# Writing the zero rows in front of the experts' regions later and in pairs, in an AdaLN mixture-of-experts block

## The chip, the cores and the metric

One core of a Trainium2 chip runs the kernel. The metric is device time in microseconds (us) of one launch, taken as the median of the runs shown. On the engines: TensorE is PE in the profile (its weight loads PEld), VectorE is DVE, ScalarE is ACT, GpSimd is POOL, and SyncE is SP, which here only issues DMAs.

## The reference

The input x has 16 steps of 256 tokens of 256 features. For each sample a small stencil with three coefficients makes `du`; the block then works on `du` as a sequence of 16 steps:

```python
hn = layernorm(x); qkv = hn @ in_proj_w.T + in_proj_b
scores = einsum('sbnd,tbnd->bnst', q, k) / 4          # causal over the 16 steps, 16 heads
x1 = x + softmax(scores) @ v @ out_proj_w.T + out_proj_b
hn2 = layernorm(x1); rp = softmax(hn2 @ router_w.T)   # 8 experts
topw, topi = top_k(rp, 2)                             # gates
y = sum over the 2 chosen experts of gate * gelu(hn2 @ w1[e]) @ w2[e]
out = input + x1 + y
```

## The kernel before

The 4096 tokens are 32 blocks of 128, one per iteration of a loop that every engine writes out for itself (`for g in range(-AHEAD, G + 3)`, with `G = 32` and `AHEAD = 4`). The work is software-pipelined. In iteration g, POOL makes the stencil sums of block g+5 (`neighbours`, L384, and `diffuse`, L392), the reciprocal deviations of blocks g+3 and g-2 (`deviation`, L401), and adds block g-2 to the output with a DMA (`add_x1`, L424). DVE normalises (`unit`, L663), which needs both deviations, and then does the products of attention; PE projects, transposes and routes; ACT moves PSUM banks and does the exponentials.

Experts work on tiles of 128 rows that all belong to one expert. Therefore each token's normalised row (256 values, its token number and 8 gates, `ROW = 265` floats, held in `ring`) is written to two places of a DRAM table `xs_d` that has one region per expert. `scatter` (L408) does this with two indirect DMAs per block. Blocks are routed in seven groups (`ENDS`, L37); `SCATTER` (L185) names the iteration in which each block's rows are scattered. Group 0 is blocks 0 to 4, scattered in iterations 10 to 12.

The last tile of an expert may reach back in front of its region. `prefix` (L417) writes rows there that hold zeros and a valid token number: eight indirect DMAs, one per expert, all from one source `zrow` with the indices `pre_row`. They count `pre_done`. `zrow` is made at the start (L380, L382, in `later_constants`) and is the last of the six buffers `xin` for loaded tiles, so SP waits for `pre_done` before it loads tile 5 there (L303).

SP loads tile j into `xin[j % 6]` (`tile_in`, L297), once tile j-6 has been added to the output; the order of SP's queue is fixed, so a load that waits holds those behind it. PE transposes the tile (`turn_in`, L950), multiplies with w1 (`up`), transposes again, and multiplies with w2 (`down`). ACT or DVE applies the gate, and POOL adds the rows to the output with one indirect DMA (`add_y`, L432), which waits until the add before it has landed. Two tiles are done in most iterations from 22 on; `WANT` (L193) fixes how many. Tiles 0 to 30 are taken inside the loop, and 31 to 70 after it. The tiles of the last group begin at `TAIL` = 47.

POOL's order in one iteration is: first waiting `add_y`, first scatter, `neighbours`, two `deviation`, `add_x1`, `diffuse`, other `add_y`, `prefix` (iteration 11 only), second scatter. Between iterations 26 and 31 the DMAs of the adds and scatters share POOL with the deviations.

The input buffers `xp` (L96) hold two loaded blocks of x. Block 31, the last one, is loaded and used up in iteration 26.

Of the kernel before, what the change touches and what calls it, by code (L numbers as in the profile page):

```python
# [9 lines left out]
I32 = mybir.dt.int32  # L10
# [7 lines left out]
def adaln_moe_block(nc, x, zX, zY, zR, ln1_w, ln1_b, in_w, in_b, out_w, out_b, ln2_w, ln2_b,  # L18
# [9 lines left out]
    S, B, H = x.shape  # L28
    NH, D = 16, H // 16
    E, _, F = w1.shape  # L30
    HC, FC = H // P, F // P
    G = B // P * S
# [12 lines left out]
    ROW = H + 1 + E  # L45
    RING = 16
    NX = 6
# [3 lines left out]
    AHEAD = 4  # L51
# [4 lines left out]
    with ctx:  # L56
        def sb(name, shape, dt=F32):
            return ctx.enter_context(nc.sbuf_tensor(name, shape, dt))
# [4 lines left out]
        def sem(name):  # L63
            return ctx.enter_context(nc.semaphore(name))
# [13 lines left out]
        iota_i = sb("iota_i", [P, TMAX + 3 * E + 1], I32)  # L78
        iota_f = sb("iota_f", [P, TMAX + 3 * E + 1])
# [3 lines left out]
        idt = sb("idt", [P, G], I32)  # L83
# [12 lines left out]
        xp = sb("xp", [P, 2, H + 2])  # L96
# [38 lines left out]
        live = sb("live", [P, TMAX])  # L135

        xin = sb("xin", [P, NX, ROW])
        zrow = xin[:, NX - 1, :]
        y = sb("y", [P, NY, H])
        xT = sb("xT", [P, HC * P])  # L140
        hm_hmT = sb("hm_hmT", [P, 2 * F])
# [13 lines left out]
        s = {n: sem(n) for n in names}  # L155
# [26 lines left out]
        ROUTE = {GROUPS[r][-1] + 4: r for r in range(NG - 1)}  # L182
# [3 lines left out]
        for g, r in ROUTE.items():  # L186
            for i, step in enumerate(GROUPS[r]):
                SCATTER[g + 2 + i // PER, i % PER] = step

        PLACES = {0: (), 1: (0,), 2: (0, 1), 3: (0, 1, 2), 4: (0, 0, 1, 2)}  # L190
        LATER = {1: (2,), 2: (3, 4), 3: (2, 3, 4)}
# [3 lines left out]
        def group_of(j):  # L195
            return [r for r in range(NG) if j >= FIRST[r]][-1]
# [13 lines left out]
        TAIL = FIRST[NG - 1]  # L210
# [17 lines left out]
        def done_in(g):  # L228

            return [j for n in range(NPLACES) for j in SLOTS.get((g, n), ()) if j >= 1]  # L230

        def added_to(j):

            return y_added[j % 2], 16 * (j // 2 + 1)
# [16 lines left out]
        def _(sp):  # L251
# [45 lines left out]
            def tile_in(j):  # L297

                if j in FIRST:
                    r = group_of(j)  # L300
                    sp.wait_ge(s["tab_ready"], r + 1)
                    sp.wait_ge(scattered[r], 32 * len(GROUPS[r]))
                if j == NX - 1:  # L303
                    sp.wait_ge(s["pre_done"], 16 * E)
                if j >= NX:
                    sp.wait_ge(*added_to(j - NX))
                row = sp.value_load(tabr[0:1, j:j + 1], min_val=0, max_val=E * CAP - P)
                sp.dma_start(xin[:, j % NX, :], xs_d[bass.ds(row, P), :]).then_inc(xin_in[j % NX], 16)

            def slot(j):  # L310
                if j == -1:
                    tile_in(0)
                    tile_in(1)
                if j + 3 < ALL:
                    tile_in(j + 3)
# [5 lines left out]
            for g in range(-AHEAD, G + 3):  # L321
                if 2 <= g + AHEAD + 1 < G:
                    load(g + AHEAD + 1)
                if 0 <= g - W1_FROM < E:
                    e = g - W1_FROM
                    sp.dma_start(w1_s[:, e * HC * F:(e + 1) * HC * F].rearrange("p (k f) -> p k f", k=HC),
                                 w1[e].rearrange("(k p) f -> p k f", p=P)).then_inc(s["w1_in"], 16)
                if 0 <= g - W2_FROM < E:
                    e = g - W2_FROM
# [16 lines left out]
        def _(pool):  # L346
            links = [0]

            def link(ins):
                links[0] += 1  # L350
                ins.then_inc(s["pool_chain"], 1)
                pool.wait_ge(s["pool_chain"], links[0])
# [11 lines left out]
            def later_constants():  # L364
                link(pool.memset(ones_b[:, :], 1.0))

                pool.affine_select(out=lower[:, :], in_=ones_b[:, :], compare_op=ALU.is_gt, fill=0.0, base=0,
                                   pattern=[[1, P]], channel_multiplier=-1).then_inc(s["const_ready"], 1)
                pool.memset(ones_r[:, :].bitcast(F32), 1.0).then_inc(s["const_ready"], 1)
                links_of = [pool.iota(iota_i[:, 0:TMAX], [[1, TMAX]], base=0, channel_multiplier=0),  # L370
                            pool.iota(iota_i[:, TMAX:TMAX + E], [[CAP, E]], base=P, channel_multiplier=0),
                            pool.iota(iota_i[:, TMAX + E:TMAX + 2 * E], [[CAP, E]], base=P - 1, channel_multiplier=-1),
                            pool.iota(iota_i[:, TMAX + 2 * E:TMAX + 3 * E], [[P, E]], base=E * CAP, channel_multiplier=1),
                            pool.iota(iota_i[:, TMAX + 3 * E:TMAX + 3 * E + 1], [[1, 1]], base=0, channel_multiplier=1),
                            *[pool.iota(idt[:, g:g + n], [[B, n]], base=p * B + c * P, channel_multiplier=1)
                              for g, c, p, n in ((0, 0, 0, FEW), (FEW, 1, 0, FEW), (2 * FEW, 0, FEW, S - FEW), (AGAIN, 1, FEW, S - FEW))]]
                links_of.append(pool.iota(iota_w[:, :].rearrange("p (a b) -> p a b", b=2), [[16, ALL // 2 + 1], [0, 2]],
                                          base=0, channel_multiplier=0))
                link(links_of[-1])
                link(pool.memset(zrow, 0.0))  # L380
                pool.tensor_copy(iota_f[:, :], iota_i[:, :])
                pool.tensor_copy(zrow[:, H:H + 1].bitcast(I32), idt[:, 0:1]).then_inc(s["const_ready"], 1)  # L382

            def neighbours(g):  # L384

# [6 lines left out]
            def diffuse(g):  # L392

                i = g % 2
                d = du[:, g % DU, :]
                pool.wait_ge(s["scaled"], 3 * (g + 1))
                link(pool.tensor_tensor(d, d, xp[:, i, 1:H + 1], ALU.mult))  # L397
                link(pool.tensor_tensor(d, d, xud[:, i, 0, :], ALU.add))
                pool.tensor_tensor(d, d, xud[:, i, 1, :], ALU.add).then_inc(s["du_ready"], 1)

            def deviation(g, k):  # L401

                pool.wait_ge(s[("stats1", "stats2")[k]], g + 1)
                i = g % 2
                link(pool.tensor_scalar(rstd[:, k, i:i + 1], mv[:, k, i, 1:2], EPS, None, ALU.add))  # L405
                pool.tensor_tensor(rstd[:, k, i:i + 1], rstd[:, k, i:i + 1], power[:, :], ALU.pow).then_inc(s[("rstd1", "rstd2")[k]], 1)  # L406
# [7 lines left out]
                    pool.indirect_dma_start(xs_d, bass.IndirectOffsetOnAxis(ap=slot_row[:, k, g:g + 1], axis=0),  # L414
                                            ring[:, g % RING, :], None).then_inc(scattered[r], 16)

            def prefix():  # L417

                pool.wait_ge(s["pre_ready"], 1)
                for e in range(E):  # L420
                    pool.indirect_dma_start(xs_d, bass.IndirectOffsetOnAxis(ap=pre_row[:, e:e + 1], axis=0),
                                            zrow, None).then_inc(s["pre_done"], 16)

# [8 lines left out]
            def add_y(j):  # L432

                pool.wait_ge(s["y_sb"], j + 1)
                if j in FIRST:
                    for i in range(4):
                        pool.wait_ge(x1_added[i], 16 * len([g for g in range(ENDS[group_of(j)]) if g % 4 == i]))
                if j >= LEFT[0]:
                    behind = pool.value_load(tabw[0:1, j:j + 1], min_val=16, max_val=16 * ALL)
                    pool.wait_ge(y_added[(j - 1) % 2], behind)  # L440
                    pool.tensor_tensor(passed[:, j:j + 1], power[:, :], power[:, :], ALU.add)  # L441
                elif j >= 1:
                    pool.wait_ge(*added_to(j - 1))
                if j >= 2:
                    pool.wait_ge(*added_to(j - 2))
                pool.indirect_dma_start(out_rows, bass.IndirectOffsetOnAxis(ap=xin[:, j % NX, H:H + 1].bitcast(U32), axis=0),  # L446
                                        y[:, j % NY, :], None, compute_op=ALU.add).then_inc(y_added[j % 2], 16)

            def scatter_at(g, n):
                if (g, n) in SCATTER:  # L450
                    scatter(SCATTER[g, n])

            neighbours(0)
            for g in range(-AHEAD, G + 3):
                adds = [j - 1 for j in done_in(g - 1)]
                for j in adds[:1]:
                    add_y(j)
                scatter_at(g, 0)
                if g == -AHEAD:
                    diffuse(0)  # L460
                    later_constants()
                if g < 0 <= g + 3:
                    deviation(g + 3, 0)
                if g + AHEAD + 1 < G:
                    neighbours(g + AHEAD + 1)
                if 0 <= g < G - 3:
                    deviation(g + 3, 0)
                if 0 <= g - 2 < G:
                    deviation(g - 2, 1)
                    add_x1(g - 2)  # L470
                if g + AHEAD + 1 < G:
                    diffuse(g + AHEAD + 1)
                for j in adds[1:]:
                    add_y(j)
                if g == list(ROUTE)[0] + 3:
                    prefix()
                scatter_at(g, 1)
            left = [j - 1 for j in done_in(G + 2)] + list(range(LEFT[0] - 1, ALL))
            while left[0] < LEFT[1]:
# [671 lines left out]
```

## Time and profile before

| | us |
|---|---|
| median of 3 runs | 724.75 (723.79 to 725.47) |
| profiled execution | 725.27 |
| its span, first to last instruction | 723.5 |
| PE busy | 585.2 |
| DVE busy | 434.1 |
| ACT busy | 349.0 |
| POOL busy | 461.3 |
| mean granted TensorE clock | 0.904 of full speed |

The span is 1.8 us shorter than the profiled execution's time. No engine is busy throughout; the shares are averages over a first stretch (to about 500 us) in which attention and experts are interleaved, and a last one in which only tiles of experts are left. A timeline row gives the start, the duration, the engine, the line, the operation with output and input, and in brackets the idle time of the engine before it with what ended that idle time. "issue" there means that no releaser is seen in the profile.

### The profile page before, as it was taken

To read this page: it belongs to the slowest core of one execution; us is meant where nothing else is said; L and a number is where in the kernel's file an instruction comes from. 1 tells how busy PE (TensorE), PEld (TensorE's weight loads), DVE (VectorE), ACT (ScalarE), POOL (GpSimd) and SP (SyncE) were. 2 spreads that over 40 slices of the span, in tenths; PEclk is the share of its full clock that TensorE was granted. 3 is DMA by queue.
4 is the path that set the end of the run, shared out by engine and by line. 5 is a ranking of instruction groups with operands and counts; after the bars stand their busy time and mean duration, and the time that the engine had idled before them with its cause. 6 is when DMAs were issued, how large, how long until landed. Compare 5 with 4: busy or idle time off the path is not lost. (4 is left out here: it accounts for less than half of the span.)

```text
span 723.5 us, 10160 instructions
## 1 busy us (share of the span) xinstructions
PE 585.2 (81%) x2640; PEld 405.8 (56%) x2640; DVE 434.1 (60%) x1028; ACT 349.0 (48%) x814; POOL 461.3 (64%) x562
## 2 busy tenths in 40 slices
PE   2567786764567969769999699999699999999992
PEld 1334454442346646546666466766477676676761
DVE  1256679974999998755895699989844000111110
ACT  4334443322433645527766456666257555444440
POOL 5787678688668565675778874584475854343432
PEclk9779997876888989889999699999899999999997
DMA  4377854233111321342324422243344544444332
GB/s 126 124 223 229 254 145 104 53 82 96 45 52 38 82 38 23 74 91 50 59 39 89 110 30 38 38 95 56 53 77 82 118 83 67 68 61 73 62 58 23
DMA packets 51547, 59.83 MB, mean 83 GB/s; under 512 B 7386, under 2 KB 47075, under 8 KB 51428
## 3 DMA queue, kind: packets, MB, share of 16 engines
q0 software_dynamic: 18288, 23.28, 20.2%
q1 hardware_dynamic: 33204, 35.91, 17.5%
q8 instruction: 24, 0.39, 0.2%
q14 instruction: 31, 0.25, 0.1%
HBM read 35.89 MB, written 27.46 MB: 88 GB/s over the span
## 5 line engine op out<-in xcount | busy, mean ns | idle before, releaser
L979 PE MATMUL b_y<-w_s,hm_hmT 128*128 x568 | 137.0, 385 | 11.8 <-ACT y L548 11.0
L446 POOL DMA_INDIRECT out_dram<-y,xin x71 | 117.9, 1660 | 34.0 <-issue 27.0
L964 PE MATMUL b_h<-w_s,xT 128*128 x284 | 134.4, 596 | 1.6 <-ACT xT L509 1.6
L979 PEld LDWEIGHTS b_y<-w_s,hm_hmT 128*128 128x128 f32 x568 | 103.5, 192 | 25.9 <-issue 14.6
L1116 PE MATMUL b_at<-ident,pv_prod 128*128 128x128 f32 x544 | 76.3, 291 | 25.8 <-DVE pv_prod L910 25.8
L681 DVE TENSOR_SCALAR y<-b_y,xin,live 128x256 f32<-128x256 f32 x24 | 13.1, 544 | 136.9 <-PE b_y L979 136.9
L910 DVE TENSOR_TENSOR pv_prod<-kv,pr 128x1024 f32<-128x1024 f32 (+2 forms) x80 | 82.6, 1074 | 19.8 <-PE b_at L1116 19.7
L844 DVE TENSOR_TENSOR qk_prod<-q,kv 128x1024 f32<-128x1024 f32 (+2 forms) x80 | 89.5, 1143 | 2.7 <-ACT kv L578 1.8
L1116 PEld LDWEIGHTS b_at<-ident,pv_prod 128*128 128x128 f32 x544 | 67.6, 154 | 30.0 <-issue 24.2
L414 POOL DMA_INDIRECT xs_d<-ring,slot_row x64 | 71.5, 1118 | 19.1 <-issue 18.2
L852 DVE TENSOR_REDUCE sc<-qk_prod 128x64 f32<-128x1024 f32 (+2 forms) x80 | 82.2, 1052 | 0.3
L1068 PE MATMUL b_qk<-wqkv,hT 128*128 128x512 f32 x128 | 80.8, 766 | 1.3 <-ACT hT L509 1.3
L405 POOL TENSOR_SCALAR rstd<-mv 128x1 f32<-128x1 f32 x64 | 28.1, 439 | 74.1 <-DVE mv L827 57.7
L964 PEld LDWEIGHTS b_h<-w_s,xT 128*128 128x128 f32 x284 | 48.9, 193 | 36.1 <-issue 36.0
L538 ACT ACTIVATE hm_hmT<-b_t 128x512 f32<-128x512 f32 x71 | 42.3, 595 | 50.1 <-PE b_t L971 49.9
L534 ACT ACTIVATE hm_hmT<-b_h 128x512 f32<-128x512 f32 x71 | 42.4, 598 | 45.1 <-PE b_h L964 45.0
L509 ACT ACTIVATE xT<-b_x,ln 128x128 f32<-128x128 f32 x142 | 57.1, 458 | 0.6 <-PE b_x L955 0.5
L1079 PE MATMUL b_tr<-ident,ring 128*128 128x128 f32 x64 | 15.2, 324 | 47.2 <-DVE ring L672 40.7
L406 POOL TENSOR_TENSOR rstd<-rstd,power 128x1 f32<-128x1 f32 x64 | 49.2, 769 | 5.3
L441 POOL TENSOR_TENSOR passed<-power 128x1 f32<-128x1 f32 x40 | 8.9, 223 | 68.2 <-DMA out_dram<-y,xin 57.5
L575 ACT ACTIVATE q<-b_qk 128x256 f32<-128x256 f32 x32 | 12.1, 377 | 83.0 <-PE b_v L1068 82.9
L397 POOL TENSOR_TENSOR du<-du,xp 128x256 f32<-128x256 f32 x32 | 29.4, 918 | 31.9 <-ACT xud L504 31.8
(168 smaller groups left out, 1038.1 us busy)
## 6 DMA issues: line engine op xcount, KB each, us to landing
xin<-xs_d SPq DMA_DIRECT2D x71, 132.5 KB, 2.2
w_s<-in_L_ffn_w_dram SPq DMA_DIRECT2D x16, 512.0 KB, 4.5
xp<-in_x_dram SPq DMA_DIRECT2D x32, 128.0 KB
xud<-in_x_dram SPq DMA_DIRECT2D x32, 128.0 KB
out_dram<-x POOLq DMA_DIRECT2D x32, 128.0 KB, 3.3
xud<-in_x_dram SPq DMA_DIRECT2D x32, 126.0 KB
out_dram<-y,xin POOLq DMA_INDIRECT x71, 3.9
xud<-in_x_dram SPq DMA_DIRECT2D x64, 1.0 KB
```

Of the source, the lines that this page charges most:

```text
L406: pool.tensor_tensor(rstd[:, k, i:i + 1], rstd[:, k, i:i + 1], power[:, :], ALU.pow).then_inc(s[("rstd1", "rstd2")[k]], 1)
L414: pool.indirect_dma_start(xs_d, bass.IndirectOffsetOnAxis(ap=slot_row[:, k, g:g + 1], axis=0), ring[:, g % RING, :], None).then_inc(scatte ...
L446: pool.indirect_dma_start(out_rows, bass.IndirectOffsetOnAxis(ap=xin[:, j % NX, H:H + 1].bitcast(U32), axis=0), y[:, j % NY, :], None, com ...
L509: ins = act.activation(dst[:, c * P:(c + 1) * P], bank[:, c * P:(c + 1) * P], ACT.Identity, scale=ln[:, 2 * k, c:c + 1], bias=ln[:, 2 * k ...
L534: act.activation(hm[:, :], b_h[:, :], ACT.Gelu).then_inc(s["gelu_done"], 1)
L844: made.append(tick(dve.tensor_tensor(qk_prod[:, m % 2, 0:(t1 - t0) * H].rearrange("p (t h) -> p t h", h=H), q[:, g % 2, :].rearrange("p (o ...
L852: summed.append(tick(dve.tensor_reduce(scv.rearrange("p n t -> p t n")[:, t0:t1, :], qk_prod[:, m % 2, 0:(t1 - t0) * H].rearrange("p (t n ...
L910: dve.tensor_tensor(pv_prod[:, at % NPV, 0:(t1 - t0) * H].rearrange("p (t n d) -> p t n d", n=NH, d=D), kv[:, values_at(v, t0):values_at(v ...
L964: mm = pe.matmul(b_h[:, :], xT[:, k * P:(k + 1) * P], w1_s[:, bass.ds(e * (HC * F) + k * F, F)], start=(k == 0), stop=(k == HC - 1))
L979: mm = pe.matmul(b_y[:, 0:H], hmT[:, k * P:(k + 1) * P], w2_s[:, bass.ds(e * (FC * H) + k * H, H)], start=(k == 0), stop=(k == FC - 1))
L1068: mm = pe.matmul(bank[:, 0:b - a], hT[:, k, :], wqkv[:, k, a:b], start=False, stop=(k == HC - 1))
L1116: mm = pe.matmul(b_at[:, k * P:(k + 1) * P], pv_prod[:, at % NPV, lo:lo + P], ident[:, :], start=(m == 0 and t == 0 and k == 0), stop=(m = ...
```

## The change

The source of the zero rows is no longer `xin[5]` but the first 265 of the 516 floats of `xp`. It is filled just before its first use, in iteration 27. The eight DMAs go out in pairs in iterations 27, 28, 30 and 31 (`G - AHEAD - 1` is 27, `G - AHEAD` is 28). SP's wait for `pre_done` moves from tile 5 to tile 47.

```diff
-        zrow = xin[:, NX - 1, :]
+        zrow = xp[:, :, :].rearrange("p i h -> p (i h)")[:, 0:ROW]
...
+        PREFIX = (G - AHEAD - 1, G - AHEAD, G - 2, G - 1)
...
-                if j == NX - 1:
+                if j == TAIL:
                     sp.wait_ge(s["pre_done"], 16 * E)
...
-                link(pool.memset(zrow, 0.0))
-                pool.tensor_copy(iota_f[:, :], iota_i[:, :])
-                pool.tensor_copy(zrow[:, H:H + 1].bitcast(I32), idt[:, 0:1]).then_inc(s["const_ready"], 1)
+                pool.tensor_copy(iota_f[:, :], iota_i[:, :]).then_inc(s["const_ready"], 1)
...
-            def prefix():
-
-                pool.wait_ge(s["pre_ready"], 1)
-                for e in range(E):
+            def prefix(i):
+
+                if i == 0:
+                    link(pool.memset(zrow, 0.0))
+                    link(pool.tensor_copy(zrow[:, H:H + 1].bitcast(I32), idt[:, 0:1]))
+                    pool.wait_ge(s["pre_ready"], 1)
+                for e in (2 * i, 2 * i + 1):
                     pool.indirect_dma_start(xs_d, bass.IndirectOffsetOnAxis(ap=pre_row[:, e:e + 1], axis=0),
                                             zrow, None).then_inc(s["pre_done"], 16)
...
-                if g == list(ROUTE)[0] + 3:
-                    prefix()
+                if g in PREFIX:
+                    prefix(PREFIX.index(g))
```

## Rows read from the trace of the kernel before

**Rows 1.** The timeline of DVE, 157 to 173 us
```profile
157.96 2.34 DVE L910 TENSOR_TENSOR pv_prod<-kv,pr 128x1024 f32<-128x1024 f32 x2
...
160.86 0.18 DVE L707 TENSOR_TENSOR odd<-logits,top 128x32 f32<-128x32 f32 x1
172.35 0.89 DVE L672 TENSOR_SCALAR ring<-x,mv,rstd 128x256 f32<-128x256 f32 x1 [11.31 <-POOL rstd L406]
```

**Rows 2.** The timeline of POOL, 153 to 173 us
```profile
153.00 1.10 POOL L421 DMA_INDIRECT xs_d<-xin,pre_row  x1 [0.17 <-issue]
...
158.24 1.76 POOL L421 DMA_INDIRECT xs_d<-xin,pre_row  x1 [0.30 <-issue]
...
164.13 0.97 POOL L414 DMA_INDIRECT xs_d<-ring,slot_row  x1 [0.30 <-issue]
...
168.91 0.21 POOL L388 COPY xp<-xp 128x2 f32<-128x2 f32 x1
...
170.00 0.61 POOL L390 TENSOR_TENSOR xud<-xp 128x256 f32<-128x256 f32 x1
170.58 0.23 POOL L405 TENSOR_SCALAR rstd<-mv 128x1 f32<-128x1 f32 x1
...
171.75 0.56 POOL L406 TENSOR_TENSOR rstd<-rstd,power 128x1 f32<-128x1 f32 x1
```

**Rows 3.** The view of line L421: nanoseconds (lowest/median/highest), starts, and landing times
```profile
L421 POOL DMA_INDIRECT xs_d<-xin,pre_row x8: 965/974/1760, 153.0 to 162.9; - x8
...
DMA to landing us min/median/max: 2.5/2.6/3.5
```

**Rows 4.** The timelines of ACT and PE, 157 to 174 us
```profile
170.64 0.51 ACT L503 ACTIVATE xud<-xud,z 128x256 f32<-128x256 f32 x1 [12.14 <-POOL xud L390]
173.29 0.69 PE L1079 MATMUL b_tr<-ident,ring 128*128 128x128 f32 x2 [11.65 <-DVE ring L672]
```

**Rows 5.** The timelines of POOL and DVE, iteration 10
```profile
124.61 1.68 POOL L390 TENSOR_TENSOR xud<-xp 128x256 f32<-128x256 f32 x1
124.60 2.50 DVE L844 TENSOR_TENSOR qk_prod<-q,kv 128x1024 f32<-128x1024 f32 x2
```

**Rows 6.** The timelines of POOL and ACT, 13 to 17 us
```profile
13.94 0.32 POOL L380 MEMSET xin<- 128x265 f32 x1
...
14.50 0.18 POOL L382 COPY xin<-idt 128x1 int32<-128x1 int32 x1
...
16.34 0.51 ACT L503 ACTIVATE xud<-xud,z 128x256 f32<-128x256 f32 x1 [0.48 <-POOL xud L390]
```

**Rows 7.** The chain that ended last: start, duration, engine or DMA, line
```profile
465.03 3.71 POOL out_dram L446
...
472.10 3.84 DMA out_dram<-y,xin
476.67 2.30 DMA xin<-xs_d
```

**Rows 8.** The timeline of PE, 479 to 514 us
```profile
479.02 0.44 PE L955 MATMUL b_x<-ident,xin 128*128 128x128 f32 x2 [0.21 <-DMA xin<-xs_d]
...
513.67 1.06 PE L1116 MATMUL b_at<-ident,pv_prod 128*128 128x128 f32 x8 [1.06 <-DVE pv_prod L910]
```

**Rows 9.** The timeline of DVE at 465 us
```profile
464.87 2.35 DVE L844 TENSOR_TENSOR qk_prod<-q,kv 128x1024 f32<-128x1024 f32 x2
```

**Rows 10.** The timeline of POOL, 449 to 520 us
```profile
449.11 1.56 POOL L446 DMA_INDIRECT out_dram<-y,xin  x1 [3.04 <-issue]
...
459.95 0.24 POOL L405 TENSOR_SCALAR rstd<-mv 128x1 f32<-128x1 f32 x1 [6.37 <-DVE mv L827]
...
501.32 2.59 POOL L446 DMA_INDIRECT out_dram<-y,xin  x1 [2.94 <-issue]
...
519.13 1.56 POOL L446 DMA_INDIRECT out_dram<-y,xin  x1 [2.96 <-issue]
```

**Rows 11.** Busy time by stretch: PE, PEld, DVE, ACT, POOL, granted clock, DMA
```profile
560.00:723.00 163.00, 150.25 (x660) 104.09 (x658) 14.62 (x33) 74.61 (x157) 76.44 (x87) 0.97 0.42 69
```

## The prediction

> **What bounds the kernel now.** I read the page first, for the shares: no engine reaches 90%, so each stretch has its own limit and I had to find those that the change touches. Second came the view of line L421, where the eight prefix DMAs are: about 0.97 us of POOL each, issued between 153.0 and 162.9 us [rows 3]. Third, the timelines around them. DVE finishes its iteration at 161.04 (160.86 + 0.18) and then does nothing for 11.31 us until POOL has written `rstd` [rows 1]. ACT is idle for 12.14 us and PE for 11.65 us in the same stretch, and both waits lead back to POOL, PE's by way of DVE [rows 4]. So here the whole core waits for one queue. POOL does the eight prefixes first, then four scatters, then `neighbours`, then the two deviations that DVE wants, and is done with these at 172.31 (171.75 + 0.56) [rows 2].
>
> The fourth reading was of the late stretch, where the DMAs go. There the chain of waits that ended last runs through POOL: an add of 3.71 us at 465.03, scatters, the next add at 472.10, its landing, and the load of tile 25 into the buffer that it frees [rows 7]. PE starts on that tile at 479.02, after a wait of 0.21 us for it [rows 8]. After 560 us, PE is busy for 150.25 of 163 us [rows 11]; that work is fixed, so a shift of its start shifts the end.
>
> **The change, part by part.**
>
> *Eight DMAs leave iteration 11.* From the start of the first prefix to that of the scatter behind it, 164.13 - 153.00 = 11.13 us go [rows 2]. If all else on POOL kept its length, `rstd` would be ready at 172.31 - 11.13 = 161.18, and DVE would wait 0.14 us instead of 11.31. But what moves forward then lies beside DVE's products. The scatters take the places of the first four prefixes, and `neighbours` begins at 168.91 - 11.13 = 157.78, while DVE multiplies from 157.96 to 160.30 [rows 1]. In iteration 10 the same POOL instruction took 1.68 us beside such products [rows 5], against 0.61 us here without them [rows 2]. The fifth prefix, started at 158.24 in the middle of the products, took 1.76 us instead of 0.97 [rows 2, 3]. The shared stretch ends at 160.30. I take 1.5 us of stretching, about 0.8 as for the fifth prefix plus 0.7 for the second addition: `rstd` at 162.7, DVE restarting there. Gain 172.35 - 162.7 = 9.6 us. The bounds are 11.1 (no stretching) and 9.0 (both additions of `neighbours` stretched by 1.07 us, as in [rows 5]). That the gain carries on I take from the order of the work: every stream after this point is fixed, all engines stand still together [rows 1, 4], and nothing downstream starts by a clock of its own. SP's loads for later blocks wait for POOL's `diffuse`, which moves with the rest, and the tiles 0 to 2 wait for the scatters, which move up by the whole 11.13 us.
>
> *A memset and a copy leave the start.* They take 0.32 + 0.18 = 0.50 us [rows 6] and stand ahead of `neighbours(1)`; ACT waits 0.48 us for that one's result [rows 6]. Gain 0.5 us; at least 0, if weights or another wait are late next.
>
> *SP's wait leaves tile 5.* Tile 5 belongs to group 1 and is loaded in iteration 17. The last prefix lands at 162.9 + 3.5 = 166.4 us at the latest [rows 3], in iteration 12. So the wait is over when SP comes to it, and its removal is worth nothing. The same wait at tile 47 stands beside the wait for the scatters of the last group, which POOL issues after the loop, behind every prefix. That wait covers it, whatever its length. SP has only later tile loads queued behind it, and PE waits for those. Without the cover, the last pair, some 3.5 us in landing [rows 3], would have to come before tile 47; it is issued ahead of the add of tile 25. Cost nothing.
>
> *The pair of iteration 27, with the new memset and copy.* They come behind the add that precedes the one at 449.11. That one waited 3.04 us for a landing [rows 10]. The new work is 0.50 us [rows 6] + 2 x 1.28 (one issue and its 0.30 us gap, [rows 2]) = 3.06 us. It fills the wait, and what sticks out is at most 0.4 us, gone again in POOL's idle 6.37 us before the next deviation [rows 10]. If that cover were gone it would cost 3.1 us. The trace has no memset of `xp`; L380 is the same shape.
>
> *The pair of iteration 28.* It stands between the add at 465.03 and the scatters, and the add at 472.10 waits for no landing there; the scatters fill the time. So the pair pushes that add, the landing, the load of tile 25 and PE by 2 x 1.28 = 2.56 us, of which PE has no slack, as it already waits 0.21 us [rows 7, 8]. PE's transposes then hold DVE's last products, so both engines move. Cost 2.5 us. Bounds: the add at 465.03 took 3.71 instead of 1.56 us, since DVE's two products ended at 467.22, and 467.22 + 1.56 = 468.78 is just its end [rows 7, 9, 10]. If it does not hit the products in the new run, 2.1 us come free, and the pair costs next to nothing; if a product of 2.35 / 2 = 1.2 us [rows 9] stretches the pair itself, 3.8 us.
>
> *The pair of iteration 30.* It fills 2.56 of the 2.94 us before the add at 501.32, which itself took 2.59 us [rows 10]. Stretched in the same way as the add at 465.03, the add could come 1 to 2 us later. PE waits 1.06 us for DVE a little later, at 513.67 [rows 8], and that slack takes nearly all of it. I take 0, and 1.2 as the upper bound.
>
> The Trainium skill (SBUF — State Buffer, Who interferes with whom) infers that a VectorE `tensor_tensor` does not hold up the descriptor generation of GpSimd's DMAs, because it takes only the read interface of the shared ports. By that rule the pairs would never be stretched, and the upper bounds of iterations 28 and 30 would be 2.6 and 0. The trace disagrees: the issue of 3.71 us ends 1.56 us after the product does.
>
> *The pair of iteration 31* has 2.56 us in 2.96 us of waiting before the add at 519.13 [rows 10]. Nothing.
>
> **Sum.** 725.27 - 0.5 - 9.6 + 2.5 = 717.7 us for an execution like the profiled one (span 723.5, and 1.8 around it). The median lies 0.5 below the profiled execution, so 717.2. A measurement of this kernel can tell about 0.2%, 1.45 us, from no change.
>
> **The rivals.**
>
> *The late pairs are free.* The pair of iteration 28 is absorbed, as the add ahead of it isn't stretched. For it: that stretching hangs on where DVE's products fall. Against it: PE's slack there was nil. 724.75 - 10.1 = 714.7 us. Chance 0.2.
>
> *The time is given back after iteration 12.* POOL falls behind again in iterations 13 to 16, with its scatters of group 1, and a second wait of DVE for `rstd` grows. Half of 9.6 us back would give 722.0 us. For it: POOL is busy for 64% of the span on the page, and it is behind again whenever it has four scatters in one iteration. Against it: nothing in those iterations has moved against its neighbours. Chance 0.1.
>
> *POOL decides in iterations 27 to 31, and the kernel is slower.* Each pair delays an add, its landing and the next tile load, and every product that it meets stretches it by 2.1 us: 4 x 2.56 + 0.5 + 4 x 2.1 = 19.1 us against 10.1 gained, so 733.8 us. It decides once none of the waits of some 3 us before the adds [rows 10] covers a pair. Three of four places speak against it. Chance 0.03.
>
> *The prefixes aren't what DVE waited for.* Then nothing moves, 724.8 us. That needs the four scatters or `neighbours` to last till 172 alone, and they take 172.31 - 164.13 = 8.2 us [rows 2]. Chance 0.02.
>
> **How the numbers follow.** The forecast has 0.65. Its own ends are 724.75 - 11.6 = 713.2 (full gain, no cost) and 724.75 - 9.0 + 3.8 + 1.2 = 720.8 with every bound bad at once; I give 713.3 to 720.4, which leaves the giving back by half and the last two rivals outside. Faster: forecast and the free pairs, and nearly all of the giving back, 0.94. Within 0.2%: 0.03. Slower: 0.03.
>
> **What would show it.** DVE's wait before `unit` at about 161 us falls from 11.3 to 1 or 2 us, with POOL's `neighbours` stretched beside the products. The first 50 us are 0.5 us shorter. In iteration 28 the two pair DMAs stand between add and scatters, and PE waits 2 to 3 us for the load of tile 25. The waits before the adds of iterations 28, 31 and 32 shrink from 3 us to nearly 0. The tail keeps its length. The forecast is wrong if DVE's next waits for POOL in iterations 13 to 16 grow by more than 2 us, if PE doesn't wait at tile 25, or if the loads of tiles 28 and 29 hold PE.

## The result, and the profile after

| | before | changed |
|---|---|---|
| median of 5 runs, us | 724.94 (723.79 to 725.47) | 718.61 (716.83 to 719.95) |
| profiled execution, us | 725.27 | 716.83 |
| its span, us | 723.5 | 715.1 |

The ratio is 0.992, with a 95% interval of 0.9899 to 0.9942. The changed kernel is faster by 0.8%, 6.3 us between the medians; 717.2 was forecast, inside 713.3 to 720.4.

From here on line numbers are those of the changed kernel: the prefix DMAs are L424, the fill L420 and L421, `add_x1` L433, `add_y` L449, DVE's `unit` L675, PE's `turn_in` L958. First DVE's timeline at the place of [rows 1]:

```profile
157.74 0.70 DVE L703 CAST idxf<-idx 128x8 f32<-128x8 uint32 x1
158.47 0.71 DVE L706 TENSOR_TENSOR oh<-iota_f,idxf 128x32 f32<-128x32 f32 x2
...
160.88 0.90 DVE L675 TENSOR_SCALAR ring<-x,mv,rstd 128x256 f32<-128x256 f32 x1 [1.37 <-POOL rstd L406]
```

The wait of 11.31 us is one of 1.37. POOL's timeline, where [rows 2] had the eight prefixes:

```profile
150.53 1.09 POOL L414 DMA_INDIRECT xs_d<-ring,slot_row  x1 [0.17 <-issue]
...
155.48 1.25 POOL L388 COPY xp<-xp 128x2 f32<-128x2 f32 x1
156.82 1.59 POOL L389 TENSOR_TENSOR xud<-xud 128x256 f32<-128x256 f32 x1
158.48 0.66 POOL L390 TENSOR_TENSOR xud<-xp 128x256 f32<-128x256 f32 x1
```

The scatters start right away, and `neighbours` is stretched beside DVE's products: the copy took 1.25 us against 0.21 [rows 2], the first addition 1.59. DVE in turn took 0.70 us for a cast that had taken 0.17. PE's wait in this place ([rows 4]) fell as well:

```profile
161.84 0.69 PE L1082 MATMUL b_tr<-ident,ring 128*128 128x128 f32 x2 [0.61 <-DVE ring L675]
```

The late stretch is where time was given back. POOL's timeline:

```profile
431.23 0.95 POOL L420 MEMSET xp<- 128x265 f32 x1
432.25 0.22 POOL L421 COPY xp<-idt 128x1 int32<-128x1 int32 x1
432.99 1.03 POOL L424 DMA_INDIRECT xs_d<-xp,pre_row  x1 [0.53 <-POOL xp L421]
...
435.63 1.71 POOL L449 DMA_INDIRECT out_dram<-y,xin  x1 [0.30 <-issue]
...
450.97 3.70 POOL L449 DMA_INDIRECT out_dram<-y,xin  x1 [0.30 <-issue]
454.98 1.46 POOL L424 DMA_INDIRECT xs_d<-xp,pre_row  x1 [0.30 <-issue]
456.74 1.00 POOL L424 DMA_INDIRECT xs_d<-xp,pre_row  x1 [0.30 <-issue]
...
460.59 1.59 POOL L449 DMA_INDIRECT out_dram<-y,xin  x1 [0.30 <-issue]
...
491.11 1.95 POOL L449 DMA_INDIRECT out_dram<-y,xin  x1 [0.30 <-issue]
...
509.70 1.60 POOL L449 DMA_INDIRECT out_dram<-y,xin  x1 [0.60 <-issue]
```

The gaps of some 3 us before three of the adds ([rows 10]) are 0.3 to 0.6 us: the pairs stand in them. In iteration 28 there was no such gap, and the pair stands between the adds of tiles 18 and 19. From the start of the one to that of the other it is 460.59 - 450.97 = 9.62 us, where it was 472.10 - 465.03 = 7.07 [rows 7]. PE's timeline shows who pays:

```profile
467.49 0.44 PE L958 MATMUL b_x<-ident,xin 128*128 128x128 f32 x2 [2.63 <-DMA xin<-xs_d]
467.77 2.56 PE L982 MATMUL b_y<-w_s,hm_hmT 128*128 x8
470.12 1.91 PE L1119 MATMUL b_at<-ident,pv_prod 128*128 128x128 f32 x8
```

PE waits 2.63 us for tile 25, where it had waited 0.21 [rows 8]. The next products are slow too. The table by stretch says why; its last three columns are the granted clock, the DMA share and GB/s:

```profile
465.00:470.00 5.00, 2.51 (x10) 2.12 (x11) 0.33 (x1) 1.30 (x3) 4.58 (x5) 0.88 0.42 81
470.00:475.00 5.00, 5.00 (x34) 4.71 (x33) 2.93 (x4) 0.58 (x3) 3.92 (x4) 0.77 0.51 107
```

PE was busy for only half of the first stretch, and the granted clock fell to 0.77 of full speed in the second, that is to the lower of its two levels (1.2 and 2.4 GHz) for part of it. From the start of the add of tile 19 to PE's start on tile 25 it is 6.90 us here (460.59 to 467.49) and was 6.92 us before (472.10 to 479.02): the load comes later because the add does.

A ledger can be made from one POOL instruction of each iteration, the DMA of `add_x1` (starts in us):

```
iteration          2       11       12       27       28       30       32
before         52.49   147.63   172.28   443.13   463.57   494.88   528.57
changed        52.02   145.16   160.81   428.84   449.50   484.67   518.69
ahead by        0.47     2.47    11.47    14.29    14.07    10.21     9.88
```

So 9.0 us come in iteration 12, 3.9 us go between iterations 28 and 30, and 8.4 us are left at the end of the span. Most of the 2.0 us between iterations 2 and 11 are not the change's, as a run below shows. Between iteration 32 and the end another 1.5 us of the lead go, where no pair stands: in this profile the granted clock fell once more there, to 0.87 between 530 and 535 us and to 0.79 between 535 and 540.

### The profile page after: what moved, and what is told of

Read it like the earlier page. It is cut to its first block and busy times, and to the rows that moved or that the text cites. A ratio compares the mean times of both kernels' runs of the same rounds, so it can differ in the third digit from the quotient of the medians.

```text
span 715.1 us, 10162 instructions
## 1 busy us (share of the span) xinstructions
PE 588.2 (82%) x2640; PEld 409.1 (57%) x2640; DVE 434.7 (61%) x1028; ACT 349.2 (49%) x814; POOL 464.4 (65%) x562
## 5 line engine op out<-in xcount | busy, mean ns | idle before, releaser
L449 POOL DMA_INDIRECT out_dram<-y,xin x71 | 119.5, 1683 | 26.1 <-issue 21.9
L1119 PE MATMUL b_at<-ident,pv_prod 128*128 128x128 f32 x544 | 79.0, 298 | 23.8 <-DVE pv_prod L913 23.8
L913 DVE TENSOR_TENSOR pv_prod<-kv,pr 128x1024 f32<-128x1024 f32 (+2 forms) x80 | 85.0, 1105 | 21.1 <-PE b_at L1119 20.9
L1119 PEld LDWEIGHTS b_at<-ident,pv_prod 128*128 128x128 f32 x544 | 70.2, 158 | 27.7 <-issue 22.0
L405 POOL TENSOR_SCALAR rstd<-mv 128x1 f32<-128x1 f32 x64 | 25.6, 401 | 69.0 <-DVE mv L830 50.7
L1071 PEld LDWEIGHTS b_qk<-wqkv,hT 128*128 128x128 f32 x128 | 30.1, 245 | 30.0 <-issue 25.5
```

The lines of the kernel that those rows point to most:

```text
L913: dve.tensor_tensor(pv_prod[:, at % NPV, 0:(t1 - t0) * H].rearrange("p (t n d) -> p t n d", n=NH, d=D), kv[:, values_at(v, t0):values_at(v ...
L1071: mm = pe.matmul(bank[:, 0:b - a], hT[:, k, :], wqkv[:, k, a:b], start=False, stop=(k == HC - 1))
L1119: mm = pe.matmul(b_at[:, k * P:(k + 1) * P], pv_prod[:, at % NPV, lo:lo + P], ident[:, :], start=(m == 0 and t == 0 and k == 0), stop=(m = ...
```

## The experiments

Each kernel is the changed kernel with one edit, but for the last. Runs that are compared closely ran on the same chip, which also ran the kernel before.

### The changed kernel again

No edit.

> The changed kernel itself, so that the kernels beside it have a base on the same chip. Expected 716.8 to 720.0 us, with PE waiting 2 to 3 us for the load of tile 25.

Measured: 718.36 us (714.94 to 720.11, 6 runs), ratio 0.992 (0.9896 to 0.9944). The changed kernel ran once more, on the same chip, beside the three kernels "Half of the DMAs back in iteration 11", "The fill back at the start" and "All eight ahead of the deviations":

> The changed kernel once more, as the base of this group: 717 to 720 us.

Measured: 717.58 us (714.73 to 718.64, 6 runs), ratio 0.9913 (0.9889 to 0.9937). PE's timeline of the first, and its table by stretch:

```profile
469.72 0.44 PE L958 MATMUL b_x<-ident,xin 128*128 128x128 f32 x2 [2.79 <-DMA xin<-xs_d]
470.00 1.89 PE L982 MATMUL b_y<-w_s,hm_hmT 128*128 x8
471.73 1.04 PE L1119 MATMUL b_at<-ident,pv_prod 128*128 128x128 f32 x8
```

```profile
465.00:470.00 5.00, 2.21 (x9) 0.90 (x7) 2.58 (x3) 2.14 (x5) 4.58 (x5) 1.00 0.48 108
470.00:475.00 5.00, 5.00 (x41) 4.74 (x40) 2.20 (x4) 0.98 (x3) 4.09 (x4) 1.00 0.55 80
```

The wait is the same, but here the clock stayed at full speed behind it. Then iterations 28 to 30 took 33.81 us, against 31.31 before and 35.17 in the first profile of the changed kernel. So the pair of iteration 28 costs 2.5 us by itself, and 1.4 us more in an execution in which the clock falls behind the wait. Two more profiles have the pair in this place, and each agrees with one of these:

```profile
470.00:475.00 5.00, 5.00 (x40) 4.43 (x39) 3.18 (x5) 1.02 (x5) 4.15 (x3) 1.00 0.51 79
```

```profile
470.00:475.00 5.00, 4.88 (x24) 4.26 (x25) 0.34 (x1) 0.81 (x2) 4.09 (x4) 0.69 0.55 80
```

The first is the changed kernel beside the other three: a wait of 2.72 us, 33.81 us for iterations 28 to 30. The second is the kernel with the fill back at the start: a wait of 2.92 us, 35.12 us.

### The pair of iteration 28, moved into another wait

```diff
+                if g == PREFIX[1]:
+                    prefix(1)
                 if g < 0 <= g + 3:
                     deviation(g + 3, 0)
...
-                if g in PREFIX:
+                if g in PREFIX and g != PREFIX[1]:
                     prefix(PREFIX.index(g))
```

> The pair of iteration 28 goes ahead of the deviations of that iteration, where POOL waits 5.3 us for DVE; the number of DMAs is unchanged. Theory (the pair pushes the add of tile 19 and with it the load of tile 25): PE's wait for tile 25 falls from 2.6 us to under 0.5, and the kernel gains 2.5 to 4 us on the changed one (714.5 to 716). Rival (the loss of 3.9 us in iterations 28 to 30 is contention or chance): no change within 1 us.

Measured: 714.66 us (711.47 to 716.2, 5 runs), ratio 0.9855 (0.983 to 0.988); beside it the changed kernel had 718.36. Its PE and POOL timelines:

```profile
467.89 0.44 PE L960 MATMUL b_x<-ident,xin 128*128 128x128 f32 x2 [0.77 <-DMA xin<-xs_d]
```

```profile
443.36 0.96 POOL L424 DMA_INDIRECT xs_d<-xp,pre_row  x1 [0.30 <-issue]
444.63 1.15 POOL L424 DMA_INDIRECT xs_d<-xp,pre_row  x1 [0.30 <-issue]
448.37 0.23 POOL L405 TENSOR_SCALAR rstd<-mv 128x1 f32<-128x1 f32 x1 [2.59 <-DVE mv L832]
```

The same eight DMAs, one pair in another place, and 3.7 us are back between the medians. The runs of each kernel spread over about 5 us, so this difference is known only to within about 3 us either way. The traces are closer to each other: iterations 28 to 30 took 31.64 us here, 2.2 less than the 33.81 above. POOL's wait before the deviation shrank from 5.32 to 2.59 us and took the pair whole. PE's wait fell to 0.77 us, a little above the 0.5 expected. The theory stands, and the rival of chance or contention falls.

### The pair of iteration 28 left out

Zero rows of two experts are not written here.

```diff
-                if g in PREFIX:
+                if g in PREFIX and g != PREFIX[1]:
                     prefix(PREFIX.index(g))
...
-                    sp.wait_ge(s["pre_done"], 16 * E)
+                    sp.wait_ge(s["pre_done"], 16 * (E - 2))
```

> The pair of iteration 28 is left out (the zero rows of two experts are not written, and the wait counts 12 transfers instead of 16 per expert pair left: 96 instead of 128). Theory: the same gain as with the pair moved ahead of the deviations, 2.5 to 4 us on the changed kernel, since the pair costs nothing there. If this one is faster by over 1 us than the moved pair, the pair ahead of the deviations still costs something. Rival: no change within 1 us.

Measured: 714.55 us (712.69 to 714.97, 4 runs), ratio 0.9863 (0.9843 to 0.9883). PE waited 0.25 us for tile 25. That is the time of the moved pair to 0.1 us, and behind the add the pair costs 3.8 us between the medians (known to within about 2 us). Ahead of the deviations no cost can be seen in the time; in the traces iterations 28 to 30 took 31.29 us here and 31.64 with the pair moved, so up to 0.4 us may be left.

### Two pairs in iteration 28

```diff
-                if g in PREFIX:
+                if g in PREFIX and g != PREFIX[2]:
                     prefix(PREFIX.index(g))
+                if g == PREFIX[1]:
+                    prefix(2)
```

> The pair of iteration 30 goes behind the pair of iteration 28, so four DMAs stand between the two adds there. Theory (each DMA in that place costs its full 1.28 us, on PE's path): PE's wait for tile 25 grows by 2.6 us to about 5.2, and the kernel is 2.5 to 3.5 us slower than the changed one (721 to 722). Rival (POOL is not on the path there): within 1 us of it, or faster, as iteration 30 loses its pair.

Measured: 723.0 us (720.65 to 725.33, 12 runs), ratio 0.9982 (0.9967 to 0.9997). Its PE timeline and table by stretch:

```profile
471.88 0.69 PE L960 MATMUL b_x<-ident,xin 128*128 128x128 f32 x2 [6.31 <-DMA xin<-xs_d]
472.36 3.62 PE L984 MATMUL b_y<-w_s,hm_hmT 128*128 x8
```

```profile
465.00:470.00 5.00, 0.57 (x2) 0.00 (x0) 1.25 (x2) 1.56 (x3) 4.28 (x5) 0.97 0.39 77
470.00:475.00 5.00, 3.12 (x9) 2.58 (x10) 0.00 (x0) 0.81 (x2) 4.09 (x5) 0.50 0.63 93
```

One pair more in this place costs 4.6 us; of the gain of about 6 us on the kernel before, 1.5 are left. The direction is the theory's, the size was expected too small (721 to 722 us): the wait grew by 3.5 us, not 2.6, since the next add was now stretched by a product of DVE (2.58 us), and the granted clock fell to 0.50 behind the long wait, where eight products took 3.62 us instead of 1.89.

### The pair ahead of the add

```diff
+                if g == PREFIX[1]:
+                    prefix(1)
                 for j in adds[1:]:
                     add_y(j)
-                if g in PREFIX:
+                if g in PREFIX and g != PREFIX[1]:
                     prefix(PREFIX.index(g))
```

> The pair of iteration 28 goes just ahead of the add of tile 18 instead of just behind it. Theory (whatever POOL issues first while DVE's two products of two inputs run is held until they end, 1.0 or 1.6 us of its own work after their end): the first DMA of the pair takes 3.0 to 3.2 us, the add of tile 18 takes 1.6 instead of 3.7, and the add of tile 19 starts as late as in the changed kernel, so the time is the changed one's, 717 to 719 us; the loads of tiles 24 and 25 both wait. Rival (the 3.7 us belong to the add, by what it moves): the pair takes 1.0 each and the add stays at 3.7.

Measured: 720.08 us (719.04 to 720.87, 5 runs), ratio 0.9953 (0.9936 to 0.9969). Its timelines of POOL and DVE:

```profile
453.49 3.15 POOL L424 DMA_INDIRECT xs_d<-xp,pre_row  x1 [0.30 <-issue]
456.94 1.99 POOL L424 DMA_INDIRECT xs_d<-xp,pre_row  x1 [0.30 <-issue]
459.24 1.62 POOL L449 DMA_INDIRECT out_dram<-y,xin  x1 [0.30 <-issue]
```

```profile
453.34 2.35 DVE L849 TENSOR_TENSOR qk_prod<-q,kv 128x1024 f32<-128x1024 f32 x2
...
456.86 1.23 DVE L849 TENSOR_TENSOR qk_prod<-q,kv 128x1024 f32<-128x1024 f32 x1
```

PE's timeline and the table by stretch:

```profile
466.08 0.69 PE L960 MATMUL b_x<-ident,xin 128*128 128x128 f32 x2 [4.01 <-DMA xin<-xs_d]
```

```profile
465.00:470.00 5.00, 3.92 (x11) 3.10 (x12) 2.83 (x3) 0.81 (x2) 4.28 (x6) 0.50 0.50 107
```

The stretching went to what now stood there. The first DMA ends 0.95 us after the two products do (456.64 against 455.69), the second 0.84 us after the next product, and the add is back at 1.62 us. So it is whatever issue stands on POOL beside DVE's products that is held, and it isn't the add's own. It isn't always held until all of them end: the fifth prefix of the kernel before, issued at 158.24 us in the first of two products of `pv_prod` (1.2 us each, from 157.96 [rows 1]), was done at 160.00, before the second one ended. What decides between one product and both is open. The time was 1 us above the range expected. The second DMA met a product as well, and the next add started 10.47 us behind the first DMA, where it is 9.62 between the two adds in the changed kernel. PE waited 4.01 us at once, for tile 24 and not for both tiles, and the granted clock behind that wait was 0.50.

### Half of the DMAs back in iteration 11

```diff
+                if j == NX - 1:
+                    sp.wait_ge(s["pre_done"], 16 * 4)
...
-                if i == 0:
+                zrow = xin[:, NX - 1, :] if i < 2 else xp[:, :, :].rearrange("p i h -> p (i h)")[:, 0:ROW]
+                if i % 2 == 0:
                     link(pool.memset(zrow, 0.0))
...
-                if g in PREFIX:
+                if g == 11:
+                    prefix(0)
+                    prefix(1)
+                if g in PREFIX[2:]:
                     prefix(PREFIX.index(g))
```

> Four of the eight DMAs go back to iteration 11 (from the last buffer of loaded rows, filled there, with the wait of tile 5 back), and the pairs of iterations 30 and 31 stay, filled in iteration 30. Theory (each early DMA lengthens DVE's wait by 1.28 us, on everyone's path): DVE's wait before it normalises in iteration 13 is 1.4 + 4 x 1.28 + 0.7 = 7.2 us at most, rather 6 us, as DVE is stretched less; as the pair of iteration 28 is gone too, 5.5 us lost and 4 won, 718.5 to 721 us. Rival (the early wait holds all eight or nothing, or time is given back behind it): under 716 or over 723 us.

Measured: 718.47 us (717.93 to 719.76, 6 runs), ratio 0.9935 (0.9915 to 0.9954). Its DVE timeline:

```profile
166.03 0.89 DVE L681 TENSOR_SCALAR ring<-x,mv,rstd 128x256 f32<-128x256 f32 x1 [7.36 <-POOL rstd L408]
```

DVE's wait is 7.36 us, 6.0 longer than the changed kernel's: a little above the 7.2 that was given as its upper end, and well above the 6 that was held more likely. The reason given for the 6 was that DVE's own work is stretched less. It was (its cast took 0.16 us), but that makes DVE ready earlier and its wait longer. From `add_x1` of iteration 11 to that of 12 it took 24.65 us before, 20.69 here and 15.65 in the changed kernel: 3.96 us between eight DMAs and four, where the fill has come into this iteration, and 5.04 between four DMAs with the fill and none. So the early wait grows with the number of DMAs and is not all or nothing. What these four cost is won back for the most part as the pair of iteration 28 is gone (iterations 28 to 30 took 31.31 us), so that the total is within 1 us of the changed kernel's.

### The fill back at the start

The memset and the copy go to the buffer `xin[5]`, where nothing reads them.

```diff
-                pool.tensor_copy(iota_f[:, :], iota_i[:, :]).then_inc(s["const_ready"], 1)
+                link(pool.memset(xin[:, NX - 1, :], 0.0))
+                pool.tensor_copy(iota_f[:, :], iota_i[:, :])
+                pool.tensor_copy(xin[:, NX - 1, H:H + 1].bitcast(I32), idt[:, 0:1]).then_inc(s["const_ready"], 1)
```

> The changed kernel with the fill of a memset and a copy put back at the start (into the last buffer of loaded rows, where nothing reads it). Theory: POOL's first 50 us are 0.5 us longer and the kernel is 0.5 us slower than the changed one, 718.7 to 719.5. Rival A (the 2.5 us by which the changed kernel was ahead at iteration 10 all come from the start, by the phase of the loop against its DMAs): 2 to 3 us slower. Rival B (the gain at the start is lost before iteration 10): no change.

Measured: 718.29 us (715.88 to 721.17, 8 runs), ratio 0.9934 (0.9911 to 0.9957), against 717.58 beside it. The 0.7 us have the right sign, but the intervals overlap, so 0.5 us aren't resolved, and rival B isn't excluded. The trace speaks for less than 0.5: `neighbours(1)` began at 14.53 us, 0.4 later than in the first profile of the changed kernel, but the `add_x1` of iteration 2 began at 52.16, only 0.05 to 0.18 later than in its three profiles, since POOL did not wait for DVE ahead of the deviation there, where it waited 0.39 us in the first of them. Rival A falls: its iteration 11 began at 146.32 us and that of the changed kernel beside it at 146.34.

### All eight ahead of the deviations

```diff
+                if g == G - AHEAD - 1:
+                    prefix(0)
+                    prefix(1)
+                if g == G - AHEAD:
+                    prefix(2)
+                    prefix(3)
                 if g < 0 <= g + 3:
                     deviation(g + 3, 0)
...
-                if g in PREFIX:
-                    prefix(PREFIX.index(g))
```

> All eight prefix DMAs go ahead of the deviations, four in iteration 27 (with the fill of 0.5 us or more) and four in iteration 28, where POOL waits 6.5 and 5.3 us for DVE. Theory (a wait of POOL for DVE takes them whole): 4 x 1.28 + 1 = 6.2 us fit into 6.5, 5.1 into 5.3, and the kernel is as fast as with the one pair moved, 713.5 to 715.5 us, and steadier. Rival (the adds before and behind are now crowded, and a deviation comes late for DVE): 1 to 3 us slower than with one pair moved.

Measured: 714.33 us (713.13 to 715.07, 5 runs), ratio 0.987 (0.9847 to 0.9892). Beside it the changed kernel had 717.58. POOL's timeline:

```profile
449.35 1.68 POOL L424 DMA_INDIRECT xs_d<-xp,pre_row  x1 [0.30 <-issue]
451.05 0.36 POOL L405 TENSOR_SCALAR rstd<-mv 128x1 f32<-128x1 f32 x1
```

DVE's timeline behind it:

```profile
453.78 0.41 DVE L679 TENSOR_SCALAR ring<-x,mv,rstd 128x256 f32<-128x256 f32 x1 [1.32 <-POOL rstd L406]
```

The wait before the deviation in iteration 28 is used up and more: the fourth DMA fell beside DVE's products and took 1.68 us, the deviations came late, and DVE waited 1.32 us for them. That part of the rival came true. Iteration 27 took 22.43 us where it takes 20.67 with the one pair moved, but iterations 28 and 29 took 29.21 instead of 31.64, so that nothing of it is left in the time. This kernel and the one with the moved pair beat both kernels, the kernel before by 1.3 to 1.5% and the changed one by 3 to 4 us; they can't be told apart from each other. With the one pair moved POOL still waits 2.59 us for DVE there, and DVE doesn't wait for POOL, so I would take that one.

### The kernel before, profiled again

No edit of the kernel before.

> The kernel before, a second profile. Theory: its waits in iterations 13 and 28 are as in the first (DVE 11.3 us for POOL, PE 0.2 us for tile 25). Open is whether its iteration 11 begins at 147.6 us again: if it begins at 145 to 146, the 2.5 us by which the changed kernel was ahead there are chance of one execution.

Measured: 724.58 us, a single run. From its view of waits, 150 to 175 us (in total, times, longest):

```profile
DVE ring L672 <- POOL rstd L406: 11.3, 1, 11.3
```

PE waited 0.7 us in all for loads of tiles between 440 and 530 us. Its `add_x1` of iteration 11 began at 146.96 us. In the ten profiles of the changed kernel and its variants it lay between 145.16 and 147.61. So the two early us of the ledger are mostly one execution's chance. The time from there to iteration 12 hardly varies: 24.65 and 24.69 us before, 15.60 to 15.66 in the nine profiles of kernels that have no prefix in iteration 11.

## Why the prediction was right

*Eight DMAs leave iteration 11: 9.6 us forecast (9.0 to 11.1), 9.0 measured.* The place, the waiting engine and the stretching beside DVE's products were as forecast, but the stretching goes both ways. POOL was held longer than the 1.5 us allowed: from the first scatter to DVE's restart it took 160.88 - 150.53 = 10.35 us, 2.1 more than the 8.2 of unstretched work. DVE's own cast and comparisons took 0.9 us more beside `neighbours`, which hides part of it: the wait that is left is only 1.37 us. The step that mis-sized it is "I take 1.5 us of stretching".

*The start: 0.5 us forecast.* The profile has `neighbours(1)` at 14.11 us instead of 14.62 and iteration 2 earlier by 0.47. In the time it can't be told from nothing, and by the one profile of the kernel with the fill put back at most 0.2 us of it reach iteration 2.

*The wait at tile 5, the new wait at tile 47, the pairs of iterations 30 and 31: nothing forecast.* The adds after them started 0.3 to 0.6 us behind POOL's last instruction, in gaps that had been idle. The kernel without its pair in iteration 28 keeps the three others; from `add_x1` of iteration 27 to that of 32 it took 85.7 us, and the kernel before 85.4. They are free to 0.3 us.

*The pair of iteration 27: nothing forecast.* The fill took 0.95 + 0.22 us and a gap of 0.53, 1.8 us with the copy's overhead from 431.23 to 432.99, not 0.5. So the next add started 5.5 us behind the one before it (430.15 to 435.63), where it had been 4.7, and 0.8 us stuck out, not 0.4. It still cost nothing, for POOL waited 5.3 us for DVE right after.

*The pair of iteration 28: 2.5 us forecast (0 to 3.8), 3.7 to 3.8 measured* against the kernels with the pair moved or left out. Its path is shown: add, landing, load, PE. 2.5 us of it are the two issues, as worked out. The rest was no term of the sum: in two of the four profiles with the pair in this place the granted clock falls behind PE's wait, which costs 1.3 to 1.4 us more. The step that failed is that a wait of PE was priced at its own length. Two such executions in four make 3.2 us on average, and what is left to 3.8 is within the spread of the runs. That it came out at the upper bound is luck: the bound stood for a product that stretches the pair, and that took only 0.46 us (the pair's first DMA, 1.46 us).

*The sum.* 0.5 + 9.0 - 3.8 = 5.7 us, where 6.3 us stand between the medians of 724.94 and 718.61, and 6.2 and 5.8 in the two other groups. The forecast of 7.6 was too high by two terms that both erred to the same side.

*The rivals.* That the late pairs are free is false for one of four places. That time is given back in iterations 13 to 16 did not happen: the lead was 11.47 us in iteration 12 and 12.76 in iteration 16, and DVE's waits for POOL in between came to 0.4 us, where they had been 0.5. PE did not wait for the loads of tiles 28 and 29 either. That the late pairs decide is false as a whole, but two pairs in iteration 28 show how near it was: that kernel is only 1.5 us faster than the kernel before.

**What holds POOL up.** The Trainium skill (SBUF — State Buffer, Who interferes with whom) infers that a `tensor_tensor` of VectorE doesn't hold up descriptor generation. The runs disagree for these indirect DMAs: 3.70 us instead of 1.6 for an add and 3.15 instead of 1.0 for a prefix, in the same place beside the same two products. The prediction saw this, though it put the end of the add 1.56 us behind the products where its rows give 1.52 (468.74 - 467.22). The same section of the Trainium skill says that a VectorE instruction with two SBUF inputs contends with a GpSimd instruction that reads SBUF. An indirect DMA takes its row numbers from SBUF, which would fit, but no run here separates that from the descriptors.

What stays open: the lead grew by 2.8 us between iterations 12 and 27 in the profile of the changed kernel. These iterations took 270.85 and 269.68 us in the two profiles of before, and 267.9 to 270.2 in the others. The spread of executions is as large as the difference, and nothing was tried on it. The tail did not keep its length either: from `add_x1` of iteration 33 to the end of the span it took 183.0 and 183.7 us in the two profiles of before, and 183.0 to 186.3 in the others. In two of these, the first of the changed kernel and the one with the pair moved, part of it is a fall of the granted clock between 530 and 540 us (to 0.79 and 0.78 in 5 us). So moving the pair takes away one place where the clock can fall, and not the others.

## What to carry to other kernels

A burst of DMA issues on an in-order queue costs nearly its full length (9.0 of 11.1 us here) to whoever waits for the next computation on that queue, though its data isn't needed for a long time. Spread it, but into the waits of the issuing engine that the timeline shows, and not only into quiet iterations: here a wait ahead of a deviation took two issues for nothing and four without a cost in the time, though the fourth made DVE wait 1.3 us, while two issues between two adds of the same iteration took back some 40% of the gain. Before placing work between two instructions of a queue, follow what the second one releases; and price a wait of TensorE at its length at least: behind waits of 2.6 to 2.9 us it cost 1.3 to 1.4 us more in two profiles of four.

## What the hardware showed that I had not expected

- The granted clock can fall after a single wait of PE of 2.6 us and need not: eight products into `b_y` took 2.56 us in one profile and 1.89 in the other behind waits of 2.63 and 2.79 us. Behind 4.01 us and 6.31 us they took 3.62 us. That this makes the times spread is not shown: the changed kernel lies between 714.7 and 720.1 us, and those with the pair moved or left out spread nearly as much, over 711.5 to 716.2.
- The same memset of 128x265 took 0.32 us at the start, and again in iteration 11 of the kernel with half of the DMAs there, and 0.95 us in iteration 27.
- POOL also slows DVE: a cast of 128x8 took 0.70 us beside a POOL addition and 0.17 us alone.
